# Wide attention: one block of softmax sums for four heads, with a quarter of the reciprocals, spread by shuffles

## The reference

```python
q = jnp.einsum('bsc,hcd->bhsd', xn, wq)          # 16 heads, 32 channels each
k = jnp.einsum('btc,hcd->bhtd', yn, wk)
v = jnp.einsum('btc,hcd->bhtd', yn, wv)
a = jax.nn.softmax(jnp.einsum('bhsd,bhtd->bhst', q, k) * D ** (-0.5), axis=-1)
if causal:                                       # L0_self: masked after the softmax
    a = a * mask
o = jnp.einsum('bhst,bhtd->bhsd', a, v)
x_out = x + o.reshape(...) @ li1_w + li1_b
```

## Time and profile before

| | |
|---|---|
| timed runs | 3508.13, 3513.26 (median), 3514.81 us |
| span of the profiled execution, first to last instruction | 3510.3 us |
| median of the timed runs over that span | 3.0 us |
| PE, busy | 2930.3 us, 83% |
| DVE, busy | 2195.9 us, 63% |
| ACT, busy | 1445.3 us, 41% |
| POOL, busy | 1300.9 us, 37% |
| mean granted TensorE clock | 0.922 |

### The profile page before, as it was taken

One profiled execution on the slowest core, in us unless ns is written; L12 is line 12 of the kernel. 1 busy time (PEld: TensorE's weight loads), 2 busy tenths in 40 slices (PEclk: granted clock), 3 DMA queues, 4 the chain that ended last, 5 costly groups with the idle time before them and its releaser, 6 DMA issues.

```text
span 3510.3 us, 87178 instructions
## 1 busy us (share of the span) xinstructions
PE 2930.3 (83%) x33512; PEld 2220.9 (63%) x33512; DVE 2195.9 (63%) x6213; ACT 1445.3 (41%) x2804; POOL 1300.9 (37%) x1385
## 2 busy tenths in 40 slices
PE   7886999869998898888879996698899877968592
PEld 5665777647776685666656664576677656856471
DVE  3565777658877544654667776444886574476544
ACT  3332444324443353434335553344666533513140
POOL 3554222320002621632223334523743325361635
PEclk9998999979998999999989997798999977988696
DMA  7000000000000231100010000221000012311232
GB/s 261 3 3 10 2 2 2 15 11 6 5 4 36 74 95 37 26 3 3 26 61 11 11 8 27 72 75 45 20 1 1 17 47 85 95 32 37 67 105 71
DMA packets 135950, 132.76 MB, mean 38 GB/s; under 512 B 25856, under 2 KB 114432, under 8 KB 134528
## 3 DMA queue, kind: packets, MB, share of 16 engines
q1 hardware_dynamic: 119168, 93.60, 8.3%
q0 software_dynamic: 16384, 33.59, 3.3%
HBM read 69.45 MB, written 57.67 MB: 36 GB/s over the span
## 4 chain that ended last, share of the span: by engine, by line
PE 63%; DVE 14%; ACT 11%; issue 7%; POOL 3%; DMA 1%; SPq 0%; POOLq 0%; DVEq 0%; ACTq 0%
PE banks L739 8%; ACT arena L1614 7%; PE banks L1414 4%; PE banks L760 4%; PE banks L1379 4%; PE banks L1432 4%; PE banks L1907 3%; PE banks L1427 3%; PE banks L1846 3%; PE banks L1878 2%; DVE arena L1637 2%; PE banks L749 2%; POOL xd L1261 2%; PE banks L1896 2%; PE banks L1484 2%
## 5 line engine op out<-in xcount | busy, mean ns | idle before, releaser
L1637 DVE TENSOR_REDUCE arena<-banks 128x16 f32<-128x2048 f32 x128 | 289.4, 2261 | 273.2 <-PE banks L1414 273.2
L2139 POOL TENSOR_TENSOR arena<-arena 128x1024 f32<-128x1024 f32 x128 | 249.4, 1955 | 292.8 <-DVE arena L2097 292.7
L739 PE MATMUL banks<-weights,arena 128*128 x1120 | 331.2, 414 | 1.1 <-issue 0.4
L1614 ACT ACTIVATE arena<-banks 128x1024 f32<-128x1024 f32 x256 | 248.2, 1021 | 173.7 <-PE banks L1432 173.7
L1647 DVE RECIPROCAL arena<-banks 128x256 f32<-128x256 f32 x128 | 223.5, 1748 | 130.8 <-PE banks L1475 70.2
L849 ACT ACTIVATE arena<-banks 128x256 f32<-128x256 f32 (+2 forms) x320 | 124.0, 387 | 360.5 <-PE banks L739 358.8
L953 POOL DMA_INDIRECT a_state<-yd,a_state x192 | 189.5, 987 | 222.2 <-DMA yd<-a_state 168.3
L1179 DVE TENSOR_TENSOR arena<-arena,banks 128x176 f32<-128x176 f32 (+2 forms) x240 | 102.4, 427 | 226.9 <-ACT arena L849 220.1
L2415 POOL TENSOR_TENSOR t_var_eps<-t_meanvar,eps 128x2 f32<-128x2 f32 (+1 forms) x132 | 26.5, 201 | 582.3 <-DVE t_meanvar L2406 582.2
L2292 POOL TENSOR_TENSOR var_eps<-meanvar,eps 128x4 f32<-128x4 f32 (+1 forms) x80 | 15.9, 199 | 564.0 <-DVE meanvar L2270 543.9
L760 PE MATMUL banks<-weights,arena 128*128 (+2 forms) x1440 | 217.2, 278 | 2.3 <-ACT a_state L861 1.7
(11 more groups left out here) (310 smaller groups left out, 7100.4 us busy)
## 6 DMA issues: line engine op xcount, KB each, us to landing
arena<-xd SPq DMA_DIRECT2D x320, 64.0 KB
xd<-zeros SPq DMA_DIRECT2D x4, 4352.0 KB, 28.8
yd<-a_state SPq DMA_DIRECT2D x120, 128.0 KB, 2.0
yd<-arena SPq DMA_DIRECT2D x40, 128.0 KB, 2.0
weights<-in_w_L_ffn SPq DMA_DIRECT2D x1, 4372.5 KB, 13.4
weights<-in_w_L_ffn SPq DMA_DIRECT2D x1, 3076.0 KB, 11.2
xd<-x_state,arena POOLq DMA_INDIRECT x192, 2.2
a_state<-yd,a_state POOLq DMA_INDIRECT x192, 2.6
```

Source lines behind the costliest of these rows:

```text
L739: ins = eng.matmul(dst, b.xt[:, k % 2, :], w[:, bass.ds(at + n * inner, inner)], start=True, stop=True)
L1614: eng.activation(b.p[:, n % 2, gs, :, :], b.s[:, gs, :, :], ACT.Exp, scale=p["scale"])\
L1637: eng.tensor_reduce(b.max[:, n % 2, :].rearrange("p (g s) -> p g s", g=4)[:, :, 0:4], b.s[:, :, :, :], AX_X, ALU.max).then_inc(sem["s_max" ...
L2139: eng.tensor_tensor(probs, probs, bcast(b.rec[:, n % 2, hs], 2, P), ALU.mult)\
```

## The change

In the wide form the sums are now built as in the dense form: `b.sums` is a block of 128x128 in the first quarter of bank 5. For quadrant g, the slot s of the four heads adds its sum into rows 8s to 8s+7 of the 32 rows, by 16 matmuls of 128 columns with the slices of `eighths`. There is one reciprocal of 128x128 into `b.rec`, ahead of `maxima(n+1)`. In `normalise` four stream shuffles on DVE spread it: shuffle s takes rows 8s to 8s+7 of each 32 rows and writes each four times, into the columns of slot s of a new buffer `b.share` (128x512). The multiplication waits for the shuffles (`p_share`, a new semaphore) and reads `b.share`. The second half reciprocal behind `maxima(n+1)` is gone. The dense form computes what it did before, through the shared functions.

```diff
-                 p_rec=2 if p["dense"] else 4, o_norm=2, o_ps=1, cleared=1 / 16)
+                 p_rec=2, o_norm=2, o_ps=1, cleared=1 / 16)
...
+        if not p["dense"]:
+            n.update(p_share=2)
...
-                self.rec = cut(BANK)
+                self.rec = cut(P)
+                if not p["dense"]:
+                    self.share = cut(BANK)
...
+                self.sums = psum[4][:, P:2 * P] if p["dense"] else psum[5][:, 0:P]
...
             def sums(n):
-                if p["dense"]:
-                    for s in range(4):
-                        for g in range(4):
-                            ins = eng.matmul(psum[4][32 * g:32 * g + 32, P:2 * P],
-                                             const("eighths")[:, 24 * s:24 * s + 32],
-                                             b.p[:, n % 2, g, s, :], start=(s == 0), stop=(s == 3))
-                    return ins
-                for g in range(4):
-                    ins = eng.matmul(psum[5][32 * g:32 * g + 32, :], const("ones"), b.p[:, n % 2, g, :, :],
-                                     start=True, stop=True)
+                for s in range(4):
+                    for g in range(4):
+                        ins = eng.matmul(b.sums[32 * g:32 * g + 32, :], const("eighths")[:, 24 * s:24 * s + 32],
+                                         b.p[:, n % 2, g, s, :], start=(s == 0), stop=(s == 3))
                 return ins
...
-            def reciprocals(n, half):
-                if half == 0:
-                    eng.wait_ge(sem["pv_ps"], after["pv_ps"](0, n + 1))
-                if p["dense"]:
-                    ins = eng.reciprocal(b.rec[:, 0:P], psum[4][:, P:2 * P])
-                else:
-                    at = slice(2 * P * half, 2 * P * half + 2 * P)
-                    ins = eng.reciprocal(b.rec[:, at], psum[5][:, at])
-                ins.then_inc(sem["p_rec"], 1)
+            def reciprocals(n):
+
+
+                eng.wait_ge(sem["pv_ps"], after["pv_ps"](0, n + 1))
+                eng.reciprocal(b.rec[:, :], b.sums).then_inc(sem["p_rec"], 1)
 
             def normalise(n):
                 i, e = n // 2, n % 2
-                cols = P if p["dense"] else BANK
-                eng.wait_ge(sem["p_rec"], after["p_rec"](0, (n + 1) * (1 if p["dense"] else 2)))
+                cols, by = (P, b.rec) if p["dense"] else (BANK, b.share)
+                eng.wait_ge(sem["p_rec"], after["p_rec"](0, n + 1))
+                if not p["dense"]:
+                    for s in range(4):
+                        ins = eng.stream_shuffle(b.share[:, s * P:(s + 1) * P], b.rec[:, :],
+                                                 [8 * s + c % 8 for c in range(32)])
+                    ins.then_inc(sem["p_share"], 1)
+                    eng.wait_ge(sem["p_share"], after["p_share"](0, n + 1))
                 eng.tensor_tensor(b.o_t[:, i % 2, e, :, :],
                                   psum[4][:, 0:cols].rearrange("p (c t) -> p c t", t=P),
-                                  b.rec[:, 0:cols].rearrange("p (c t) -> p c t", t=P), ALU.mult)\
+                                  by[:, :].rearrange("p (c t) -> p c t", t=P), ALU.mult)\
                    .then_inc(sem["o_norm"], 1)
...
                 if n and not p["dense"]:
-                    reciprocals(n - 1, 0)
+                    reciprocals(n - 1)
                 if n + 1 < batch:
                     maxima(n + 1)
                 if n:
-                    reciprocals(n - 1, int(not p["dense"]))
+                    if p["dense"]:
+                        reciprocals(n - 1)
                     normalise(n - 1)
```

More of the change, by code:

```diff
@@ L1708, in dve_heads @@
                 dve_late_rows(eng, l, n)
[L1709 to L1713, removed]
+            reciprocals(batch - 1)
             normalise(batch - 1)
```

## The result

| | before | after |
|---|---|---|
| median of 11 runs | 3513.26 us | 3506.78 us |
| least to most | 3504.90 to 3517.76 | 3500.18 to 3511.67 |
| span of the profiled execution | 3510.3 | 3504.0 |

In a second session the same kernel gave 3505.07 against 3512.49 us, 0.9979 (0.9970 to 0.9988). All runs are in the fast state. The change is a small gain; in the first session it lies just inside the 0.2% that the prediction took for no change, in the second just outside.

The account below looks back on a forecast made before the run. PE and ACT's exponentials bound the steady loop, so only drains gain: 4.9 (drains) + 0.7 (maxima) - 0.5 (sums) + 1.3 (clock) = 6.4 us less, from 3513.3 to 3507 us; range 3501 to 3514 us.

Parts of the forecast that it names:

- The bound: Steady stretches of both wide attentions: PE and ACT's exponentials make the chain, no DVE instruction in it.
- Rival E: Wide attention loop: reciprocals bound it, each of 60 elements gains 1.3 us, 78 us less, 3435 us; chance 0.02.
- C: Sums group in every element: PE becomes slower; at 0.20 us past the cover, 7 us slower, 3520 us; chance 0.05.
- Sums on PE, +0.13 us: Each wide element: new sums 1.01 against 0.88 us, hidden in steady state, 0.5 us lost at the stage ends.
- The shuffles, 1.2 us: DVE ahead of the multiplication: four shuffles with pattern loads, tail and new wait cost 1.2 us an element.
- The maxima, 0.17 us, four times: Elements 2 and 31 of each wide stage: maxima start earlier behind the shorter reciprocal, 0.7 us less in all.
- The clock, half of 2.6 us: Last element's sums and products in both wide stages: 2.6 us less if the clock stays up; 1.3 us counted.
- rival B: Wide drains: shorter pauses keep the clock up for last elements and output projections, 7.7 to 11.5 us less; chance 0.38.
- A: The forecast: gain at the drains alone, clock up in one place or none, 4 to 7 us less; chance 0.49.

Follow-up runs that it names:

- kernels with three new elements and with 29: New form in elements 29 to 31 of each wide stage alone: 3509.57 us, 0.9986 to the kernel before; in elements 0 to 28 alone: 3515.95 us, 1.0005.
- double shuffles: Whole change plus four more shuffles an element into a buffer that nothing reads: 3511.94 us, 0.9990 to the kernel before.
- double sums: Whole change with the 16 matmuls of the wide sums done twice: 3538.77 us, 1.0070 to the kernel before.
- kernel with filled pauses: Whole change plus matmuls that nothing reads in PE's two pauses of each wide drain: 3505.34 us, 0.9980 to the kernel before.
- early layer norm: Whole change, next stage's first layer norm moved to behind element 29's multiplication in wide stages: 3498.33 us, 0.9961 to the kernel before; again 3501.68 us, 0.9972.

## Why the prediction was right, point by point

**The bound.** Right. The steady loop is PE and the exponentials, and it kept its 18.66 us a group. The kernels with three new elements and with 29 show it from both sides, the double shuffles and the double sums measure the room: over 0.8 us on DVE, 0.34 us on PE. Rival E (the reciprocals bound the loop) is out, and C (PE slower in every element) with it.

**Sums on PE, +0.13 us.** Wrong size: +0.02 us. I read the 1.01 us of the earlier trace rows, where another kind of matmul (128x128 tiles) follows the sums. Between the sums and products of the wide form, both 128x32 tiles, 0.90 us lie from start to start. In steady state the trace says the same thing with PE's wait, 0.27 us, where I had expected 0.15. It cost nothing either way.

**The shuffles, 1.2 us.** Right kind, a little dear: 0.94 us from the start of the first shuffle to that of the multiplication (646.65 to 647.59). The 0.28 us of a single statistics instruction, for which the prediction names, does not stand in those rows; the trace of the kernel before has it (280 ns, the mean of 368). The pitch of 0.19 us taken from the statistics instruction measured 0.21, and the patterns, taken at 0.07 us each, show 0.01 and cost no time of their own. The rule of the Trainium skill (VectorE: DVE Perf Modes, "The DRAIN you can't avoid") would have given 1.4 us as the prediction read it. The same section adds that a next instruction that is not held starts earlier, and with that the trace agrees: each shuffle starts 0.08 us before the end of the one ahead. So a drain element gained 3.40 - 1.94 = 1.46 us, not 1.23: 5.8 us for the four, forecast 4.9. PE's pauses went to 0.83 and 2.84 us, forecast 1.1 and 3.1.

**The maxima, 0.17 us, four times.** Right: from the start of the scores to the maxima's transposition 3.84 us before (628.28 to 632.12) and 3.67 after (631.38 to 635.05). In all four places PE's pause ahead of their transposition fell by 0.16 or 0.17 us: for element 2 from 0.75 to 0.58 us in L0_self and from 0.48 to 0.32 in L0_cross, for element 31 from 2.66 to 2.50 us in both.

**The clock, half of 2.6 us.** The full amount came: the last element's sums and products took 1.99 us in both stages, before 2.90 and 3.54, so 2.5 us. The last output projection got faster in L0_self, 3.77 to 2.65 us, and hardly in L0_cross, 3.58 us. Of that, from the multiplication's start to the tail addition's, 0.2 us a stage arrived (4.63 us before in both, 4.43 and 4.46 after). Already before the change the layer norm was done only 0.1 us ahead of the projection (652.99 and 653.08), so a faster projection had little more to give. Its row in the kernel before, to be read beside the last of the earlier trace rows:

```profile
651.87 1.12 DVE L2316 TENSOR_SCALAR z<-xo_state,meanvar,rstd 128x128 f32<-128x128 f32 x4
```

Here the prediction had a gap: it counted nothing for this term, but for its uncertainty, and as rival B it priced it at 1.9 us a stage. It says of what DVE's queue holds behind the multiplication that in steady state nobody waits for it, and says nothing of the drain. There the next stage's layer norm stands ahead of the tail addition. The kernel with filled pauses shows that B could not have got those 3.8 us, and the one with the early layer norm what stood in the way. One piece of evidence for B was read too narrowly: the pause of 2.66 us did leave the clock up in L0_cross, but in L0_self the same pause ahead of 632.12 was followed by a fall, in the kernel before (columns as in the earlier trace rows). The prediction has no row of it.

```profile
632.00:634.00 2.00, 1.88 (x37) 1.79 (x41) 1.97 (x2) 0.28 (x1) 0.00 (x0) 0.68 0.04 8
634.00:636.00 2.00, 2.00 (x40) 1.75 (x40) 0.36 (x1) 0.11 (x1) 0.00 (x0) 0.50 0.00 0
```

**What the sum left out.** 5.8 + 0.7 - 0.1 + 2.5 + 0.4 = 9.3 us; L0_self and L0_cross together lost 4.24 + 5.68 = 9.9 us. The missing 0.6 us lie at the start of L0_cross: up to the maxima of its element 4 it is 38.26 us after and 39.15 before, 0.9 us less, of which the maxima explain 0.17. The kernel with only the last three elements new has the old form there and still took 38.63 us, so part of the gain comes from the clock and not from the new instructions: in the second 6 us of the stage it is 0.50 before and 0.78 after. Of the two MLPs behind, the first took 2.0 us more and the second 2.0 less. There too the granted clock differs (windows of the kernel after, at the start of the first MLP and of the second; the column ahead of the last two is the clock):

```profile
652.00:656.00 4.00, 2.53 (x6) 1.55 (x7) 2.19 (x15) 2.06 (x2) 1.21 (x2) 0.50 0.50 140
656.00:660.00 4.00, 4.00 (x6) 1.51 (x5) 2.25 (x14) 1.37 (x2) 1.21 (x2) 0.52 0.41 158
1063.00:1067.00 4.00, 2.88 (x9) 1.48 (x10) 2.26 (x15) 2.97 (x4) 1.21 (x2) 1.00 0.60 179
```

and of the kernel before at the same two places:

```profile
654.00:658.00 4.00, 3.07 (x10) 1.40 (x9) 2.24 (x15) 3.43 (x4) 1.21 (x2) 1.00 0.67 225
...
1068.00:1072.00 4.00, 3.07 (x7) 1.64 (x8) 2.29 (x15) 2.06 (x2) 1.21 (x2) 0.50 0.66 213
```

Before, the low stretches fell on the end of L0_self, and on the end of L0_cross and the start of the second MLP; after, on the start of the first MLP and on the last projections. In the first drain the low stretch was moved, in the second shortened: it is over when the second MLP starts.

**The total.** Forecast 3507 us, measured 3506.8 and in the second session 3505.1. That it fits to 0.2 us is luck: the local gain was 9.9 us, not 6.4, and the rest of the program scatters by more than that difference from execution to execution. By the stages the result lies in rival B's 7.7 to 11.5 us and not in A's 4 to 7, and the first part of B came in full, the clock of both last elements; by the totals it lies at A's upper end or just above it. A and B are not told apart by the time, only by the rows. What was right is the kind of result, a few us from the drains, and nothing from the halved reciprocals.

**What stays open.** The early layer norm gave 4.2 us in the four stages in both of its profiled executions, and ratios of 0.9961 and 0.9972 against 0.9979 for the change. By the stages most of it is where the low clock falls, so I can't say that another kernel, or another length of any stage ahead, would keep it. Why the 2.66 us pause ahead of the transposition of the last maxima is followed by a low clock in L0_self and not in L0_cross was not settled either. As measured, the change with the early layer norm in the wide stages is the fastest kernel of this study; its interval and that of the change overlap.

## What to carry to other kernels

A busy engine with the costliest group of instructions may still be worth only its drains: before work is taken off an engine, ask in how many repetitions the chain of waits passes through it, here 4 of 64. When a drain is shortened, look at the queue of the same engine for work of the next stage that stands ahead of the last step, since that becomes the wait. For changes below 0.3%, compare stage lengths between landmarks of the traces, which repeat within 0.2 us here for one and the same kernel, and keep the clock's share apart, because the low stretch may only move to another stage.

## What the runs showed of the hardware

- A stream shuffle of 128x128 f32 takes 0.29 us, 0.21 us from start to start, with a new pattern for each at no visible cost.
- Matmuls of 128x32 tiles with 128 columns cost in a row what 512-column ones do for the same columns: 0.90 against 0.88 us for 2048 columns over four column groups, although there are four times as many weight loads.
- DVE's TENSOR_SCALAR from SBUF to SBUF, four of 128x128, took 2.71, 2.74 and 2.55 us beside POOL's affine select, 1.12 us without it. A stream shuffle beside the same affine select took its usual 0.29 to 0.30 us, in three kernels (at 639.71, 640.14 and 639.94 us). Why the one is slowed and the other is not, no run here shows.
- A shorter pause in a drain does not always remove the low clock behind it. With PE's pauses cut from 2.29 to 0.83 and from 4.29 to 2.84 us, a stretch at 1.2 GHz turned up at the start of the next stage in one of two drains (clock 0.50 from 652 to 656 us, before 1.00) and was gone from there in the other (1.00, before 0.50).
